# Beginning the slot layer earlier in the third phase of an eight-group transformer kernel

## The reference

```python
x = x + _L2_xattn_ref(_layernorm(x), ctx, ctx, ...)     # 16 heads of 8
x = x + _L2_ffn_ref(_layernorm(x), slot_init, ...)      # the slot layer
x = x + _L3_xattn_ref(_layernorm(x), ctx, ...)          # 16 heads of 64
x = x + _L3_ffn_ref(_layernorm(x), sw1, ..., rb)        # 8 experts, top 2

# the slot layer, per token x (after a layernorm):
h = gelu(concat(x, slot_mean) @ w1.T + b1)
logits = (h @ w2.T + b2) / (abs(tau) + 0.1)             # 64 slots
alpha = softmax of the 8 largest logits, 0 elsewhere
slot_input = alpha.T @ x;  gi = slot_input / alpha.sum(tokens)
r, z, n = a GRU cell of gi and the slots (sigmoid, sigmoid, tanh)
S_new = (1 - z) * n + z * slots
out = (alpha @ (S_new @ wv.T + bv)) @ wo.T + bo
```

## Time and profile before

| what | value |
|---|---|
| median of 3 runs | 2442.34 us (2441.18 to 2447.15) |
| the profiled execution's own time | 2443.1 us |
| its span, first to last instruction | 2441.3 us |
| mean granted TensorE clock | 0.882 of full speed |
| TensorE, VectorE, ScalarE, GpSimd busy | 80%, 62%, 53%, 26% of the span |
| half steps 41 to 102 (all units, slot layers of groups 2 to 5 and the start of the experts) | 1365.9 to 1943.5 us |
| half steps 103 to 150 (a unit in every second one) | 1943.5 to 2310.8 us |

### The profile page before, as it was taken

How to read it: one execution, slowest core, us unless ns; L and a number is a source line. 1 busy time by engine, 2 the same in 40 slices (tenths; PEclk the granted TensorE clock), 3 DMA queues, 4 the chain that set the end, 5 groups by cost and what they waited for, 6 DMA issues and landing times.

```text
span 2441.3 us, 49251 instructions
## 1 busy us (share of the span) xinstructions
PE 1941.3 (80%) x17184; PEld 1549.6 (63%) x17184; DVE 1508.2 (62%) x3920; ACT 1294.3 (53%) x4431; POOL 628.8 (26%) x626
## 2 busy tenths in 40 slices
PE   3887977878689878447788889898998887878864
PEld 2666866667577656135666667776776766666664
DVE  5886865757567788555566665655656554555442
ACT  2755554545455656435576756565665654544421
POOL 0002021311411220013233343242342423232331
PEclk9877999879899987557799999898998999999987
DMA  7002444343344200310000011122221222222253
GB/s 212 28 16 89 121 123 128 101 125 106 112 139 120 67 22 6 113 41 17 26 6 13 6 56 50 50 66 77 66 66 49 74 76 79 74 83 78 76 153 107
DMA packets 125124, 184.17 MB, mean 75 GB/s; under 512 B 10320, under 2 KB 82064, under 8 KB 124624
## 3 DMA queue, kind: packets, MB, share of 16 engines
q1 hardware_dynamic: 116688, 164.23, 22.8%
q0 software_dynamic: 8192, 16.79, 2.4%
HBM read 145.52 MB, written 35.45 MB: 74 GB/s over the span
## 4 chain that ended last, share of the span: by engine, by line
PE 34%; DVE 9%; ACT 6%; issue 6%; POOL 1%; DMA 1%; SPq 0%; DVEq 0%; ACTq 0%; POOLq 0%
PE ps L1610 6%; PE ps L1859 4%; ACT pb L1999 4%; PE ps L1838 3%; PE ps L1845 3%; PE ps L1648 3%; PE ps L1632 2%; DVE nm L2351 2%; PE ps L1639 2%; PE ps L1621 2%; PE ps L1817 2%; PE ps L1666 1%; DVE hT L2142 1%; ACT pt L2007 1%; DVE hT L2137 1%
## 5 line engine op out<-in xcount | busy, mean ns | idle before, releaser
L1999 ACT ACTIVATE pb<-ps,nm 128x128 f32<-128x128 f32 x1024 | 363.3, 377 | 264.1 <-DVE nm L2351 263.9
L2040 POOL TENSOR_TENSOR pb<-pb,rcs 128x512 f32<-128x512 f32 x256 | 266.7, 1042 | 803.8 <-DVE rcs L2340 802.3
L964 ACT ACTIVATE pb<-pb,nm 128x128 f32<-128x128 f32 x1024 | 313.0, 391 | 92.6 <-DVE nm L1187 90.3
L2351 DVE TENSOR_REDUCE nm<-ps 128x8 f32<-128x1024 f32 x128 | 156.1, 1219 | 138.3 <-PE ps L1845 71.5
L2360 DVE COPY pt<-ps 128x512 f32<-128x512 f32 x128 | 88.3, 690 | 223.0 <-PE ps L1859 223.0
L1999 ACT ACTIVATION_READ_ACCUMULATOR pb<-ps,nm 128x1 f32 x1024 | 222.0, 217 | 0.0
L1859 PE MATMUL ps<-w,pb 128*128 128x128 f32 x1024 | 173.9, 297 | 49.8 <-ACT pt L2007 42.7
L1610 PE MATMUL ps<-hT,big 128*128 128x128 f32 x960 | 151.8, 308 | 54.7 <-DVE hT L2142 44.1
L851 PE MATMUL ps<-w,pb 128*128 128x128 f32 x1024 | 168.9, 309 | 28.7 <-ACT pb L964 18.6
L1610 PEld LDWEIGHTS ps<-hT,big 128*128 128x128 f32 x960 | 135.4, 216 | 80.1 <-DVE hT L2142 58.4
L1859 PEld LDWEIGHTS ps<-w,pb 128*128 128x128 f32 x1024 | 128.2, 153 | 80.8 <-issue 68.0
(11 more groups left out here) (365 smaller groups left out, 4387.8 us busy)
## 6 DMA issues: line engine op xcount, KB each, us to landing
big<-in_we SPq DMA_DIRECT2D x92, 514.0 KB
big<-in_we SPq DMA_DIRECT2D x120, 384.0 KB
big<-sorted_in SPq DMA_DIRECT2D x8, 960.0 KB, 6.5
sorted_out<-big SPq DMA_DIRECT2D x28, 256.0 KB
sorted_in<-big SPq DMA_DIRECT2D x4, 1472.0 KB, 12.1
sorted_out<-h_all SPq DMA_DIRECT2D x16, 256.0 KB
hidden<-h_all SPq DMA_DIRECT2D x7, 512.0 KB, 2.9
h_all<-hidden SPq DMA_DIRECT2D x7, 512.0 KB, 3.9
```

The lines of the kernel that those rows point to most:

```text
L964: m = a.activation(pb[:, n % 2, k * S:(k + 1) * S], pb[:, n % 2, k * S:(k + 1) * S], ACT.Exp, bias=nm[:, n % 2, k:k + 1])
L1999: m = a.activation(pb[:, n % 2, e * S:(e + 1) * S], ps[:, score_bank(n) + half, k * S:(k + 1) * S], ACT.Exp, bias=nm[:, n % 2, e:e + 1], a ...
L2040: g_.tensor_tensor(p4, p4, r4.unsqueeze(2).to_broadcast([P, 4, S]), ALU.mult).then_inc(n2["p_normed"], 1)
L2351: v.tensor_reduce(nm[:, n % 2, :], ps[:, bank:bank + 2, :].rearrange("p a (j k) -> p (a j) k", k=S), AX, ALU.max, negate=True).then_inc(n2 ...
```

## The change

The half steps at which the slot layer begins are moved for groups 2 to 7: by six half steps for groups 2 to 6, by eleven for group 7.

```diff
         L2_AT = [[NU * g + u if g < FILL else NU * FILL + 2 * NU * (g - FILL) + 2 * u for u in range(NU)] for g in range(NG)]
         L3_AT = [[L2_AT[FILL][0] + 1 + 2 * IC3 * g + 2 * c for c in range(IC3)] for g in range(NG)]
         ROW_AT = [[at[2 * b + 1] + (4 if g == FILL - 1 else 3) for b in range(G)] for g, at in enumerate(L2_AT)]
-        SLOT_AT = [10, 22, 41, 57, 73, 89, 105, 121]
+        SLOT_AT = [10, 22, 35, 51, 67, 83, 99, 110]
         MOE_AT = [at[IC3 - 1] + 4 for at in L3_AT]
```

## The result

The changed kernel took 2464.3 us (median of 10 runs, 2446.0 to 2473.9), the kernel before 2441.8 us on the same chip (10 runs, 2435.5 to 2447.6): ratio 1.0083, 95% interval 1.0056 to 1.0109 (a ratio is estimated over all runs, so it need not be the quotient of the two medians). It is slower by 22.5 us, where +7.6 was forecast. The time lies at the upper end of the stated range, but above the 2443 to 2459 of the forecast itself: the range holds it only because it was drawn out to the second rival's 2464. The clock after is 0.878.

What follows compares the result with a forecast made beforehand. TensorE was taken as the bound, busy 80% of the span, with time lost to waits and low clock. New price 91.4 us less old price 83.8 gave +7.6, so 2450 us was predicted; range 2428 to 2464, rounded up.

Steps and rivals of the forecast that it cites:

- the forecast itself: Whole kernel: +7.6 us from the summed prices, 2450 us predicted, own range 2443 to 2459; chance 0.33.
- second rival: Half step 69's stand brings as long a low stretch as 76 has: 14.4 us more, 2464; chance 0.07.
- The stand at L1584: Half step 69: prologue transposes wait for the Gelu behind L2024; TensorE stands 3.1 us, in each of groups 2 to 5.
- L1791 and L1598: Groups 3 to 5: query matmul waits for VectorE's reading of logits, 0.5 us; transposition waits behind VectorE work, 1.4 us.
- The relief: Half steps the slot layer leaves get shorter: 75-76 from 32 to 27 to 30 us, 79 to 82 from 39.7 to 32 to 36.
- The clock: TensorE may run at its low level after the 3.1 us stand: 2.0 us each for groups 3 to 5, bounds 0 and 6.8.
- The old price: Slot layer's cost where it stood: 83.8 us over groups 2 to 7, bounds 70.4 and 97.3; group 7 at 11.5.
- Groups 6 and 7: Half steps 99 to 132: new prices 10.8 and 9.8 us, 20.6 against 24.4 before, a gain of 3.8.
- surcharge of 2.0: Group 6, above the 8.8 us base: 1.0 for a full TensorE, 1.0 for statistics before the router's apply on VectorE.
- first rival: Low clock of 75-76 and 81-82 goes: faster, to 2430, if under about 5 us low remain in 68 to 72; chance 0.30.
- third rival: No difference: waits come as summed but the clock stays (+0.6 us, 2443), or old and new collisions weigh the same; chance 0.30.

Runs made afterwards that it cites:

- tanh: Gelu replaced by tanh, needing no table load: in the changed kernel 2429.48 us, ratio 0.9963 to the kernel before; in the kernel before 2435.25 us, 0.9950.
- Gelu in the middle: Changed kernel with the Gelu in ScalarE's place 1 instead of place 2 of the same half step: 2353.69 us, ratio 1.0024 to the kernel before.
- second profile: Another profiled execution of the changed kernel, unaltered, on another chip: 2459.04 us, ratio 1.0091 to the kernel before.
- filler: Changed kernel with value matmuls L1666 issued four times over in half steps 37, 53, 69 and 85: 2340.94 us, ratio 0.9977 to the kernel before.
- value copy first: Changed kernel with ScalarE's value copy L1921 put in front of the Gelu of the same half step: 2471.15 us, ratio 1.0068 to the kernel before.

## Why the prediction was right, and where its size was off

- **The stand at L1584: right.** Forecast 3.1 us for each of four groups, measured 3.12 in group 4 and 11.5 us over the four. The reader of the bank was named, and tanh and the Gelu in the middle shrink the stand as its two causes (the load, the place behind L2024) say.
- **L1791 and L1598: right.** 0.5 was summed for the query matmul, it waits 0.61. The tile's transposition waits 2.29 us instead of 0.71, 1.6 where 1.4 was summed.
- **The relief: about right.** 75-76 were to fall from 32 to 27 to 30 and came to 30.21 (26.57 in the second profile); 79 to 82 were to fall from 39.7 to 32 to 36 and came to 32.91.
- **The clock: the term that was mis-sized.** "I take 2.0" for each of groups 3 to 5; with the filler 6.1 us of low-clock cost go away in group 4, and half step 70 took 16.9 us where about 12 was forecast, the 12.5 that it takes with the filler. The upper bound of 6.8 was much nearer. Not all of it hangs on the stand: of the 13.7 us low in 68 to 72, one stretch of 10.2 follows the stand and one of 3.4 follows L1598's wait of 2.29 us. The reason given for 2.0, that the work around half step 70 is only partly TensorE's, was wrong: TensorE is busy 14.03 of its 16.93 us, at a clock of 0.70, so nearly every microsecond at the low level is one of work at half speed. Half step 38 says the same for group 2: 1.0 was taken; its 9.4 us at the low level are worth 4.7.
- **How these fit the table.** For group 4 the clock term was 4.1 too small, and the net is 5.3 - 2.3 = 3.0 over the forecast, so the relief must have been about 1 us larger than summed; this last is a remainder, from one pair of profiles, and not measured by itself. In low-clock time the two even out in this pair: half steps 68 to 72 have 13.7 us of it that were not there, 73 to 83 have 13.7 less. What is left over is idle time: TensorE is idle 9.35 us instead of 4.72 in 68 to 72, and 13.67 instead of 12.31 in 73 to 83, where the waits for `combine` have stayed. So the change trades low stretches for others and adds the stand; where the new ones do not come, as with the filler, 68 to 83 take 156.7 us against 157.1 before, and the kernel is no slower than before.
- **The old price was read off a row with an accident in it.** The 11.5 us of a group rest on 85.91 us for half steps 137 to 148 without a slot layer. These hold 10.2 us at the low level (6.8 in the 97.42 us that they were taken from). In both profiles of the changed kernel, where these instructions stand in the same order, they have none and take 81.32 us. Taking half of the low-clock time out of both rows, as an estimate, the price of group 7 is about 13, not 11.5, and five groups were priced by it: an error of some 7 us. It went the other way than the clock's (three times 4.1 and once 3.7, 16 us) and hid part of it: 7.6 + 16 - 7 is 16.6, between the +14.3 and the +21.3 that half steps 33 to 132 have in the two profiles.
- **Groups 6 and 7: a wait that was not seen, in a sum that came out.** They were to gain 3.8 us, and the traces give 0.6 to 6.3. But "Group 6 meets no prologue: 8.8 + 1.0 + 1.0" leaves out a wait that costs more than the whole surcharge of 2.0, so that the sum agrees is in part luck. In the odd half step 101 the Gelu with its load stands in front of the value copy L1921, and the first matmul of attention 3 in 102 waits for that copy, in the kernel after:

```profile
1966.09 1.64 PE L1632 MATMUL ps<-h_all,big 128*128 128x512 f32 x2 [1.90 <-ACT h_all L1921]
...
2093.25 2.07 PE L1610 MATMUL ps<-yTm,big 128*128 128x128 f32 x8 [2.82 <-DVE hT L2142]
```

Half step 102 grows from 8.35 to 17.14 us with 8.0 at the low level, and is as long in two more traces (17.75 and 17.45). The value copy first shows that this copy is the greater part of it. Where later half steps give it back was not taken apart. The second row is in 115-116, for group 7, with 4.6 us low behind it (1.7 in the second profile).
- **Of the rivals,** the second was the nearest in its time, 2464: its price of 4.8 more in each of three groups is near the 4.1 measured, and its "as long a low stretch as 76 has" came in two pieces (10.2 and 3.4 us, where 76 had one of 13.6). Its mechanism was the right one; it was held for unlikely at 0.07. The first rival's condition, fewer than 5 us of low clock left in 68 to 72, failed with 13.7. What was right without luck is the stand, its place and its length; that the time fell into the range is owed to this rival's having been put into it. On the third rival, the Trainium skill (TensorE: Matmul & The Clock Gate, Why this matters for your kernels) wants no idle gap over about 3 us; behind the 3.12 us stand the trace agrees, but half step 102 went to the low level for 6.8 us behind a wait of 1.90 us, and half step 70 with tanh for 3.4 us behind L1598's wait of 2.29 us. In the filler kernel the same wait of 2.29 us in half step 70 had no low stretch behind it, and the tanh kernel's 1.66 us none either. The measurement decides: that no single gap was over 3 us was no protection here.
- **What stays open.** 6.3 of the 21.0 us of span lie before the third phase, where the instructions are the same and kernels of two other batches took 1063.8 to 1089.1 us. The clock has the greatest part in it: TensorE is busy 814.7 us there in the profile of before and 822.5 in that of after, with 312.6 and 333.0 us at the low level. In the second profile of the changed kernel the third part is +9.7 and not +16.7 over before, and of the kernel before itself there is only the one. So the size of the loss is known to its interval, 0.6 to 1.1% (13.7 to 26.6 us), and not better; that it is one, and that without the low stretches in the prologue's half steps the change is no longer slower, is shown. What set off the low stretches of half steps 139 and 145 in the one profile of before was not tried; of the twelve other traces, in which these half steps have the same order, five have 3.4 us low in 137 to 148 and seven none.

## What to carry to other kernels

When a step moves, find each shared buffer whose reader is then another engine's slow instruction, here a bank that only comes free after a table load and a Gelu, and ask what TensorE's next instruction waits for. Price a stand on a busy TensorE at its own length plus the low stretch that may follow, at full half-speed cost if TensorE is loaded there; here a stand of 3.1 us came to 9.2, with the 6.1 that the filler got back (the shorter of its two low stretches followed another wait). And try the neighbouring places too: six, seven and nine half steps gave +0.8%, -0.2% and -0.7%, with the same instructions. Before a row serves as the price of something, look how much low-clock time it holds.

## What was not expected of the hardware

- **Useless work made the changed kernel faster.** With some 2.7 us of repeated matmuls in each of four stands the third part has 74.8 us of low-clock time, where the two profiles of the changed kernel have 122.9 and 102.4, and is 21.9 and 14.9 us shorter.
- **The low level lasted with TensorE busy.** In the earlier trace rows it held for 13.64 us with TensorE busy for 13.32, and behind the stand of half step 69 for 10.2 us with 9.6 busy.
- **The chips differ, and only in part of the program.** The kernel before took 2347.97 us on one chip and 2440.15 and 2451.29 on two others. Up to the third phase they need 986 to 989 us on the one and 1064 to 1089 on the others, over the kernels run, with 244 to 250 and 313 to 373 us at the low level. In the third phase half steps 137 to 148, where they hold no low-clock stretch, take 81.28 to 81.32 us on all of them.
- **The table load has no hole behind it.** The Gelu starts 0.02 us after its load ends, as it did before.
